# Quantised attention: rounding the softmax weights on GpSimd instead of VectorE, with GpSimd's program unrolled over the steps

## The reference, cut to what matters

```python
q = _fq_sym(q, axis=-1); k = _fq_sym(k, axis=-1); v = _fq_sym(v, axis=2)
attn = jnp.einsum('bhqd,bhkd->bhqk', q, k)
attn = jax.nn.softmax(attn.astype(jnp.float32), axis=-1)
attn = _fq_unsigned(attn, axis=-1)      # s = max/255; q = clip(round(x/s), 0, 255)*s
out = jnp.einsum('bhqk,bhkd->bhqd', attn, v)
```

## Time and profile before

| | |
|---|---|
| median of 3 runs | 1971.04 us (1963.87 to 1972.36) |
| profiled execution: its own time | 1975.08 us |
| its span in the trace | 1973.3 us |
| busy over the span | PE 1499.5 us (76%), DVE 1246.8 (63%), ACT 938.2 (48%), POOL 253.8 (13%) |
| the units of the quantised attention | about 1325 to 1671 us of the span |

### The profile page before, as it was taken

One profiled execution on the slowest core, in us unless ns is written; L12 is line 12 of the kernel. 1 busy time (PEld: TensorE's weight loads), 2 busy tenths in 40 slices (PEclk: granted clock), 3 DMA queues, 4 the chain that ended last, 5 costly groups with the idle time before them and its releaser, 6 DMA issues.

```text
span 1973.3 us, 27083 instructions
## 1 busy us (share of the span) xinstructions
PE 1499.5 (76%) x9126; PEld 1038.9 (53%) x9146; DVE 1246.8 (63%) x2789; ACT 938.2 (48%) x2777; POOL 253.8 (13%) x451
## 2 busy tenths in 40 slices
PE   5874554577776886785699999747888888997886
PEld 4652433355554554554466776424444445775664
DVE  4677886578777777776223322359888988663342
ACT  2543754465555554563235534136766776322111
POOL 0000000243333333331000000000000000000000
PEclk7876776799999899899699989866565655896879
DMA  5102001000000000000500000000000000000000
GB/s 230 68 3 86 0 0 46 1 1 6 1 0 5 0 3 3 1 1 13 212 1 1 0 0 0 11 6 1 1 0 0 0 0 37 7 0 1 0 0 21
DMA packets 13573, 37.98 MB, mean 19 GB/s; under 512 B 2201, under 2 KB 8866, under 8 KB 10802
## 3 DMA queue, kind: packets, MB, share of 16 engines
q1 hardware_dynamic: 13490, 36.99, 4.9%
HBM read 35.94 MB, written 1.05 MB: 19 GB/s over the span
## 4 chain that ended last, share of the span: by engine, by line
PE 45%; DVE 28%; ACT 11%; POOL 8%; issue 7%; DMA 1%; DVEq 0%; POOLq 0%; ACTq 0%; SPq 0%; another core or an unknown queue 0%
POOL small L1222 4%; PE PS L2101 4%; PE PS L2713 3%; PE PS L2081 3%; ACT work L1296 3%; DVE small L2221 3%; PE PS L1747 2%; DVE small L1159 2%; PE PS L1703 2%; DVE work L2231 2%; POOL small L1220 2%; POOL small L1221 2%; PE PS L1682 2%; PE PS L1692 2%; PE PS L1727 2%
## 5 line engine op out<-in xcount | busy, mean ns | idle before, releaser
L1296 ACT ACTIVATE work<-PS,small 128x128 f32<-128x128 f32 x256 | 90.4, 365 | 202.9 <-DVE small L1160 202.9
L2221 DVE TENSOR_REDUCE small<-PS 128x1 f32<-128x1024 f32 x128 | 156.3, 1221 | 16.4 <-PE PS L2081 11.4
L2166 ACT ACTIVATE work<-PS,small 128x1024 f32<-128x1024 f32 x128 | 154.8, 1209 | 24.3 <-DVE small L2223 23.2
L206 POOL TENSOR_TENSOR rstd<-moments,eps 128x1 f32<-128x1 f32 x56 | 12.4, 221 | 1139.3 <-DVE moments L186 1139.3
L2101 PE MATMUL PS<-ident_b,work 128*128 128x128 bf16 x1024 | 121.0, 292 | 43.0 <-DVE work L2231 36.8
L1331 PE MATMUL PS<-late 128*128 128x512 f16 x384 | 103.1, 409 | 32.9 <-DVE late L1115 28.2
L2081 PE MATMUL PS<-early,work 64*128 64x512 bf16 x256 | 120.0, 567 | 5.2 <-ACT work L2166 3.5
L2101 PEld LDWEIGHTS PS<-ident_b,work 128*128 128x128 bf16 x1024 | 91.0, 132 | 48.4 <-DVE work L2231 37.1
L2159 ACT COPY work<-PS 128x512 f32<-128x512 f32 x128 | 75.0, 586 | 66.3 <-PE PS L2101 66.3
L1222 POOL TENSOR_TENSOR small<-small,minus_half 128x4 f32<-128x4 f32 x96 | 96.8, 1008 | 7.5
L1408 PE MATMUL PS<-work 128*128 128x256 f32 x256 | 73.8, 413 | 31.3 <-DVE work L1115 15.0
(11 more groups left out here) (397 smaller groups left out, 3737.4 us busy)
## 6 DMA issues: line engine op xcount, KB each, us to landing
late<-in_C_proj SPq DMA_DIRECT2D x1, 4096.0 KB, 12.1
ctxT<-in_ctxT SPq DMA_DIRECT2D x24, 128.0 KB, 2.5
late<-in_C_q SPq DMA_DIRECT2D x1, 2048.0 KB, 8.5
late<-in_C_qx SPq DMA_DIRECT2D x1, 2048.0 KB, 12.6
late<-in_F_w SPq DMA_DIRECT2D x2, 1024.0 KB
late<-in_B_gate SPq DMA_DIRECT2D x1, 1024.0 KB, 8.7
late<-in_B_up SPq DMA_DIRECT2D x1, 1024.0 KB, 10.5
late<-in_B_down SPq DMA_DIRECT2D x1, 1024.0 KB, 12.6
```

The lines of the kernel that those rows point to most:

```text
L1296: last = nc.scalar.activation(C_[g]["p"][:, h, :], PS[:, SBANK, h * P:(h + 1) * P], ACT.Exp, scale=DC ** -0.5, bias=small[:, g, 8 + h:9 + ...
L2166: nc.scalar.activation(E_[g]["e"], banks(g, 2), ACT.Exp, scale=small[:, g, h:h + 1], bias=small[:, g, 48 + h:49 + h], accum_out=small[:, g ...
L2221: ch.link(nc.vector.tensor_reduce(small[:, g, 80:81], banks(g, 2), AX.X, ALU.max))
```

## The change

`whole` moves from DVE to POOL, the same operation on the same data with the same waits. POOL's part of the sublayer is no longer a loop over the steps but written out for all four steps. On DVE the function that held the rounding keeps only the reciprocal of the sums at the last head of each sequence, with its own wait for the exponential.

```diff
-            E_pipeline(pool, ch, lambda ch: None, [(None, extra)])
+            def whole(ch, i, u):
+                g = u % G
+                pool.wait_ge(E_exp.sem, E_exp.nth(i, u))
+                if u >= G:
+                    pool.wait_ge(E_pturned.sem, E_pturned.nth(i, u - G))
+                nc.gpsimd.tensor_scalar(E_[g]["pb"], E_[g]["e"], MAGIC, MAGIC - 1.0, ALU.add, ALU.subtract).then_inc(E_pb.sem, 1)
+
+            stages = [(2, whole), (None, extra)]
+            E_slots(ch, 0, range(0, E_DEPTH), stages)
+            ch.restart()
+            for i in range(STEPS):
+                E_slots(ch, i, range(E_DEPTH, E_UNITS + E_DEPTH), stages)
+                ch.restart()
...
-            def whole(ch, i, u):
+            def sums(ch, i, u):
                 h, g = head_of(u), u % G
-                dve.wait_ge(E_exp.sem, E_exp.nth(i, u))
-                if u >= G:
-                    dve.wait_ge(E_pturned.sem, E_pturned.nth(i, u - G))
-                nc.vector.tensor_scalar(E_[g]["pb"], E_[g]["e"], MAGIC, MAGIC - 1.0, ALU.add, ALU.subtract).then_inc(E_pb.sem, 1)
                 if h == HE - 1:
+                    dve.wait_ge(E_exp.sem, E_exp.nth(i, u))
                     ch.link(nc.vector.reciprocal(small[:, g, 16:32], small[:, g, 64:80]))
...
-            E_pipeline(dve, ch, lambda ch: None, [(None, reads), (2, whole), (None, extra), (0, maximum)])
+            E_pipeline(dve, ch, lambda ch: None, [(None, reads), (2, sums), (None, extra), (0, maximum)])
```

## The result

The changed kernel takes 2125.81 us (median of 4 runs, 2119.22 to 2132.58) against 1970.12 us before: a ratio of 1.081, 95% interval 1.0777 to 1.0842. It is 8% slower; 1957 us with a range from 1943 to 1992 was forecast.

The account below looks back on a forecast made before the run. PE was taken to bound the plain units at the lower clock. Terms -13 - 2.5 + 1.5 = -14 us took the 1971.0 us median to 1957 us, range 1943 to 1992.

Parts of the forecast that it names:

- What POOL gets: Price of one 1024-column rounding on POOL: 1.02 us taken, 0.78 lower and 2.33 upper bound, from cast and memset rows.
- The rival of the slow POOL: POOL's rounding over 1.30 us sets the pace; break-even at 1.52 us, at worst +52 us, 2023 us; chance 0.18.
- the loop: Exponential, POOL's rounding (T us), transposes, copy, next exponential of that sequence: 3.00 + T us per two units, 4.02 at T = 1.02.
- PE bounds the plain units at the lower clock: In attention units without other work, at clock 0.50, PE runs without a gap: 2.15 us each, freed DVE time worth 0.
- The blocks: Other work at fixed slots between attention units, where DVE is late: 34 blocks x 0.60 = 20 us at most, 13 taken.
- The small scaling: Rival: DVE's L2223 after each maximum waits for POOL's rounding in every unit: +28 us, 1999 us; chance 0.04.
- The sum of -14 us: Whole forecast change: -13 where DVE is late for other work, -2.5 at the upper clock, +1.5 for POOL's queue.
- a discount of a third: Of at most 20 us gained where DVE is late for other work, only two thirds, 13 us, were counted.
- a loss behind the norm's roots: On POOL, two root pairs (1.6 us) once a step delay the rounding behind them: 3 x 0.5 = 1.5 us lost.
- 34 x 0.60 + 4: Undiscounted gain: 0.60 us at each of 34 slots of other work, plus 0.18 x 23 = 4 us at the upper clock.
- more gain through the clock: Rival: granted clock 1.00 throughout, plain units at 1.80 us, 44 us; a gain of over 28 us had chance 0.05.
- The rival at the blocks: POOL and DVE hold each other up during other work: 10 us of the gain gone, 1967 us, no change; chance 0.20.

Follow-up runs that it names:

- The four runs with a short rounding: Changed kernel with POOL rounding 256 columns, multiplying by 1 and adding 1, or writing f16; earlier kernel with DVE rounding 64 columns: ratios 0.9883, 0.989, 0.9876, 0.9869.
- the f16 version: Changed kernel with POOL multiplying by 1, adding 1024 and writing f16, weights, transposes, values and identity in f16: 1950.73 us against 1977.36 before, ratio 0.9876.

## Why the prediction was wrong

**The step that failed** is the price of POOL's instruction in "What POOL gets": 1.02 us, nearest to the cast and the memset, and 2.33 us as the upper bound with "nothing of the cast is fixed". It measured 3.636. Both values came from rows of instructions without arithmetic, and the bound assumed that two operations cost at most what a cast without a fixed part would. The 128-column cast was the right row for a cast (1.037 at 1024 columns) and said nothing of a TENSOR_SCALAR; a bound "from above" must come from rows that have the operation, or be left open. The only rows of POOL with arithmetic had 1 to 4 columns.

The Trainium skill (GPSIMD Engine Reference, Performance versus the Vector engine) gives 1.03 cycles per element at 1.2 GHz for bodies of up to two operations, and I let it stand beside my 1.02. The runs here agree for the cast and for multiply and add (1.04 and 1.05 us for 1024 columns), and differ for add and subtract: 3.3 ns a column is four cycles of 1.2 GHz for each element, an estimate from that clock. The measurement decides.

**The rival of the slow POOL** was right in kind, at a chance of 0.18, and too small: its worst case was 2023 us. It also named only the loop, (3.00 + T)/2 = 3.32 us a unit at T = 3.63. With every unit on POOL, POOL's own queue is longer than that, 3.63 + 0.08 = 3.71, which is what the trace shows; beyond T = 2.84, where T + 0.08 passes (3.00 + T)/2, the prediction should have had this second bound.

**What held.** *PE bounds the plain units at the lower clock, and freeing DVE gives them nothing:* with POOL at 1.05 us or with DVE's rounding nearly gone, the last exponentials stayed 2.15 us apart. *The loop of 3.00 + T:* 6.62 measured for 6.63, and 4.91 for 4.92. *The blocks are where freed DVE time counts:* the interval over a quantisation of the queries was 4.33 us before in the first step and 3.64 with 256 columns on POOL, 0.69 less where 0.6 was forecast. *Unrolling costs nothing:* ratio 0.9996. *The small scaling is not held up:* L2223 took 214 ns before and its successor L2235 214 ns after.

**What was mis-sized.** The sum of -14 us held a discount of a third and a loss behind the norm's roots. The four runs with a short rounding gave -23 to -27 us between first and last exponential, the f16 version the least with 309.44 us: about the full 34 x 0.60 + 4 = 24, without a discount. With T = 1.02 the time would have been near 1946, an estimate, inside the range. That the sum comes out so well is in part luck. Each of these is one trace, and the stage's mean granted clock was 0.61 to 0.63 in them, against 0.59 or 0.60 in the three traces with the whole rounding on DVE, so some of the gain may be the clock's; I had put more gain through the clock aside because nothing gives PE more work. And with multiply and add on POOL the interval over a quantisation did not shrink at all (below), while the whole gained 24 us.

**The rival at the blocks** was real, and it ate less than the 10 us that I had given it: with multiply and add on POOL the units took 308.52 us, with 64 columns on DVE 305.65. Two groups of DVE instructions before (the multiplication by the reciprocal sums, with two SBUF inputs, and the rounding of the queries, with constants):

```profile
L2207 DVE TENSOR_SCALAR work<-work 128x256 bf16<-128x256 f32 x18 | 4.2, 288 | 0.2
L2255 DVE TENSOR_TENSOR work<-work,small 128x256 f32<-128x256 f32 x8 | 3.4, 424 | 0.3
```

The same two after the change, where POOL hardly rests (the window of this view ends at 1800 us, before the last two of L2264, which took 0.42 us each):

```profile
L2219 DVE TENSOR_SCALAR work<-work 128x256 bf16<-128x256 f32 x18 | 7.6, 474 | 0.2
L2264 DVE TENSOR_TENSOR work<-work,small 128x256 f32<-128x256 f32 x6 | 7.0, 1171 | 0.2
```

And the first of them with multiply and add on POOL:

```profile
L2219 DVE TENSOR_SCALAR work<-work 128x256 bf16<-128x256 f32 x18 | 8.5, 524 | 0.2
```

That is 0.24 us more each for 18 instructions, 4 us in all, and the interval over a quantisation is 4.42 us there, against 3.65 where the rounding is 64 columns on DVE and 3.64 with 256 columns of the slow form on POOL.

How long a DVE instruction is held up goes by the form on POOL too. With multiply and add, the three roundings of the queries took 1.41 us together at all six places, 0.70 before; the first of them began 0.20 us into POOL's instruction and got done after its end:

```profile
1371.96 1.07 POOL L2191 TENSOR_SCALAR work<-work 128x1024 bf16<-128x1024 f32 x1 [0.60 <-ACT work L2166]
1372.16 1.41 DVE L2219 TENSOR_SCALAR work<-work 128x256 bf16<-128x256 f32 x3
```

With add and subtract, POOL was in one rounding from 1393.54 to 1397.17 (the second of the three merged below), and DVE worked in the middle of it at its full speed:

```profile
1389.84 11.05 POOL L2191 TENSOR_SCALAR work<-work 128x1024 bf16<-128x1024 f32 x3
...
1394.94 0.43 DVE L2217 TENSOR_TENSOR work<-work,small 128x256 f32<-128x256 f32 x1
...
1395.40 0.70 DVE L2219 TENSOR_SCALAR work<-work 128x256 bf16<-128x256 f32 x3
```

It did so at four of the six places; at the other two the three took 2.4 us. The Trainium skill (SBUF — State Buffer, Who interferes with whom) has such a DVE instruction and a GpSimd instruction exclude one another for the whole instruction. The rows with multiply and add agree; those with add and subtract do not, since the hold-up is not for the whole of the 3.63 us, and the measurement decides. What in the slow form lets DVE through stays open.

## What to carry to other kernels

Before work is moved to GpSimd, measure the very instruction there: the pair of operations changed its time by a factor of 3.5 at the same size and types, and the rewrite to a fast pair, with f16 in place of bf16, turned 8% slower into 1.2% faster. Write down both bounds for the engine that receives the work, its own queue (T and a handover per unit) and the loop of dependences through it (here 3.00 + T for two units). And look where the engine that is relieved is late: here 87 us of freed busy time were worth about 25, none of it in the plain units that PE bounded at the lower clock.

## What I had not expected of the hardware

A GpSimd TENSOR_SCALAR of 128x1024 took 1.05 us with multiply and add, multiply and multiply, or add and multiply, 2.77 with one multiplication or one addition alone, and 3.63 or more with add and subtract, add and add, subtract and add, multiply and subtract, multiply and maximum, or maximum and minimum; an addition of two f32 tiles of that size took 2.21. Add and subtract of 256, 512 and 1024 columns took 1.08, 1.92 and 3.63 us, which is a line of 0.22 us and 3.3 ns a column; 128 columns lie above it with 0.97, where the cast of 128 columns took 0.29.
